# Attention with its probabilities turned by DMA: one transfer per plane for both row tiles, instead of one per plane and tile

## The reference

```python
qkv = mix_precision_matmul(x, weight_qkv)       # x here is layernorm(x)
q, k, v = jnp.split(qkv, 3, axis=-1)
q = q / jnp.sqrt(jnp.asarray(d, dtype=q.dtype))
qk = jnp.einsum('bqd,bkd->bqk', q, k)
s = jax.nn.softmax(qk, axis=-1)
y = jnp.einsum('bqk,bkd->bqd', s, v)
return jnp.matmul(y, out_w.T) + out_b
...
x = x + _layernorm(_L0_attn_ref(_layernorm(x), ...))
x = x + _layernorm(_L0_ffn_ref(_layernorm(x), ...))
```

## Time and profile before

| what | value |
|---|---|
| median of the timed runs | 859.05 us (858.09, 859.05 and one at 1708.93) |
| the profiled execution's own time | 856.61 us |
| its span | 854.8 us |
| granted TensorE clock, mean | 0.976 |
| TensorE, matmuls | 809.6 us busy, 95%, x5870 |
| VectorE | 693.6 us, 81% |
| ScalarE | 503.1 us, 59% |
| GpSimd | 434.0 us, 51% |
| DMA queue of SyncE | 54.8% of 16 engines' span |
| pt_hi<-p_hi, pt_lo<-p_lo | 64 transfers each, 4.5 and 3.7 us from issue to landing (medians) |

### The profile page before, as it was taken

The page is one execution under the profiler, slowest core; times in us unless marked ns, Lnnn a source line. Parts: engine busy times, 40 slices in busy tenths (PEclk is TensorE's granted clock), DMA queues, the critical chain, the costliest instruction groups (busy, mean ns, idle before and its releaser), DMA issues.

```text
span 854.8 us, 16115 instructions
## 1 busy us (share of the span) xinstructions
PE 809.6 (95%) x5870; PEld 614.0 (72%) x5870; DVE 693.6 (81%) x1767; ACT 503.1 (59%) x634; POOL 434.0 (51%) x638
## 2 busy tenths in 40 slices
PE   4779999999999999999999999999999999999963
PEld 3437777777777777777777777777777777778853
DVE  4687798877899888877988888888877777898683
ACT  3275566655566675655676756656766565566532
POOL 1100254655656566556546665564456555645872
PEclk8799999999999999999999999999999999999977
DMA  6568854546656646566455666675435455545301
GB/s 178 112 139 144 177 137 107 125 106 141 148 118 117 142 107 143 117 124 148 106 117 119 142 150 118 124 142 99 106 88 105 113 110 123 125 99 108 79 12 38
DMA packets 336574, 101.58 MB, mean 119 GB/s; under 512 B 310256, under 2 KB 336240, under 8 KB 336496
## 3 DMA queue, kind: packets, MB, share of 16 engines
q1 hardware_dynamic: 336496, 100.56, 54.8%
HBM read 18.75 MB, written 8.39 MB: 32 GB/s over the span
## 4 chain that ended last, share of the span: by engine, by line
PE 88%; DVE 5%; POOL 2%; ACT 1%; issue 1%; DMA 1%; SPq 1%; ACTq 0%; POOLq 0%; DVEq 0%
PE M L885 7%; PE M L886 7%; PE M L887 7%; PE S L917 6%; PE Y L936 6%; PE Y L939 6%; PE Y L937 6%; PE Y L938 6%; PE Y L940 6%; PE S L921 6%; PE S L918 6%; PE S L920 6%; PE S L919 6%; PE M L965 2%; DMA xs<-in_L_attn_x 1%
## 5 line engine op out<-in xcount | busy, mean ns | idle before, releaser
L681 DVE TENSOR_SCALAR_CACHE_REDUCE probs<-S 128x512 f32<-128x512 f32 x256 | 173.0, 679 | 94.9 <-PE S L921 94.4
L514 ACT ACTIVATE probs<-probs,exp_bias,kappa 128x2048 f32<-128x2048 f32 x64 | 134.0, 2094 | 70.7 <-DVE exp_bias L692 70.7
L697 DVE TENSOR_TENSOR p_lo<-probs,p_hi 128x2048 f16<-128x2048 f32 x64 | 166.0, 2594 | 1.9 <-ACT p_hi L475 1.9
L936 PE MATMUL Y<-pt_hi,planes 128*128 128x256 f16 x512 | 139.6, 273 | 0.3 <-issue 0.3
L939 PE MATMUL Y<-pt_lo,planes 128*128 128x256 f16 x512 | 139.6, 273 | 0.0
L937 PE MATMUL Y<-pt_lo,planes 128*128 128x256 f16 x512 | 139.6, 273 | 0.0
L940 PE MATMUL Y<-pt_hi,planes 128*128 128x256 f16 x512 | 139.6, 273 | 0.0
L938 PE MATMUL Y<-pt_hi,planes 128*128 128x256 f16 x512 | 139.6, 273 | 0.0
L475 ACT ACTIVATE p_hi<-probs 128x2048 f16<-128x2048 f32 x64 | 122.0, 1906 | 1.2
L917 PE MATMUL S<-turned,q_hi 128*128 128x512 f16 x256 | 98.8, 386 | 10.3 <-DVE probs L681 7.7
L532 ACT ACTIVATE att<-att,ashift,arstd 128x256 f32<-128x256 f32 x62 | 33.9, 593 | 111.6 <-POOL ashift L387 111.6
(11 more groups left out here) (135 smaller groups left out, 2078.9 us busy)
## 6 DMA issues: line engine op xcount, KB each, us to landing
x_res<-in_L_attn_x SPq DMA_DIRECT2D x32, 256.0 KB, 3.8
out_x<-gate SPq DMA_DIRECT2D x32, 256.0 KB, 3.0
xs<-in_L_attn_x SPq DMA_DIRECT2D x32, 128.0 KB, 3.1
xs<-in_L_attn_x SPq DMA_DIRECT2D x16, 256.0 KB, 4.0
pt_hi<-p_hi SPq DMA_TRANSPOSE x64, 4.5
pt_lo<-p_lo SPq DMA_TRANSPOSE x64, 3.7
pt_hi<-in_L_attn_weight_qkv SPq DMA_DIRECT2D x3, 128.0 KB, 2.8
pt_hi<-in_L_attn_weight_qkv SPq DMA_DIRECT2D x1, 256.0 KB, 3.1
```

What stands on the lines that cost most here:

```text
L681: dve.tensor_scalar(probs[:, t, c * BLK:(c + 1) * BLK], S[k % RING][:, :], 1.0, None, ALU.mult, ALU.max, accum_out=chunk_max[:, t, c:c + 1 ...
L697: dve.tensor_tensor(p_lo[:, t, :], probs[:, t, :], p_hi[:, t, :], ALU.subtract).then_inc(p_lo_made, 1)
L936: pe.matmul(to[:, 0, :], low, p_h, start=first, stop=False, skip_group_check=True)
```

## The change

`turn_probs(h, plane)` turns one plane of both tiles in one transfer of 32 blocks: `p_hi` [128, 2 x 2048] to `pt_hi[:, a]`, and likewise for the low plane. For this the turned planes are laid out tile by tile, [128, 2, 2, 16, 128] with tile before key tile. The high plane's transfer is due in slot 9 and waits for both tiles' p_hi, the low one's in slot 11 as before, waiting for both tiles' p_lo. There is one semaphore per plane. `probs_high` waits for the high plane's transfer of the block before (for either tile), `probs_low` of tile 0 for the low plane's. `attend` waits for both planes, and its moving operand is now two runs of 128 elements, 2048 elements (4 KB) apart.

```diff
-    TURN_P = (7, 11)
+    TURN_P = (9, 11)
...
-        pt_hi = sb("pt_hi", [P, 2, NKT, ROWS], F16)
-        pt_lo = sb("pt_lo", [P, 2, NKT, ROWS], F16)
+        pt_hi = sb("pt_hi", [P, 2, RT, NKT, P], F16)
+        pt_lo = sb("pt_lo", [P, 2, RT, NKT, P], F16)
...
-            def turn_probs(h, t):
-                a, cols = h % 2, slice(t * P, (t + 1) * P)
-                if h == 1 and t == 0:
+            def turn_probs(h, plane):
+
+                a = h % 2
+                if h == 1:
                     sp.wait_ge(w_turned, 7)
-                if h >= 2 and t == 0:
+                if h >= 2:
                     sp.wait_ge(pv_done, h - 1)
-                sp.wait_ge(p_hi_made, h * RT + t + 1)
-                sp.dma_start_transpose(pt_hi[:, a, :, cols], p_hi[:, t, :]).then_inc(pt_in[t], 16)
-                sp.wait_ge(p_lo_made, h * RT + t + 1)
-                sp.dma_start_transpose(pt_lo[:, a, :, cols], p_lo[:, t, :]).then_inc(pt_in[t], 16)
+                if plane == 0:
+                    sp.wait_ge(p_hi_made, (h + 1) * RT)
+                    sp.dma_start_transpose(pt_hi[:, a].rearrange("p t k q -> p (t k) q"),
+                                           p_hi.rearrange("p t n -> p (t n)")).then_inc(pt_hi_in, 16)
+                else:
+                    sp.wait_ge(p_lo_made, (h + 1) * RT)
+                    sp.dma_start_transpose(pt_lo[:, a].rearrange("p t k q -> p (t k) q"),
+                                           p_lo.rearrange("p t n -> p (t n)")).then_inc(pt_lo_in, 16)
...
             def probs_high(h, t):
                 act.wait_ge(exp_made, h * RT + t + 1)
                 if h >= 1:
-                    act.wait_ge(pt_in[t], 32 * h)
+                    act.wait_ge(pt_hi_in, 16 * h)
...
             def probs_low(h, t):
                 dve.wait_ge(p_hi_made, h * RT + t + 1)
+                if h >= 1 and t == 0:
+                    dve.wait_ge(pt_lo_in, 16 * h)
...
-                    for t in range(RT):
-                        pe.wait_ge(pt_in[t], 32 * (h + 1))
+                    pe.wait_ge(pt_hi_in, 16 * (h + 1))
+                    pe.wait_ge(pt_lo_in, 16 * (h + 1))
...
-                p_h, p_l = pt_hi[:, h % 2, kt, :], pt_lo[:, h % 2, kt, :]
+                p_h, p_l = pt_hi[:, h % 2, :, kt, :], pt_lo[:, h % 2, :, kt, :]
```

More of the change, by code:

```diff
@@ L241, in sandwich @@
         exp_made = sem("exp_made"); p_hi_made = sem("p_hi_made"); p_lo_made = sem("p_lo_made")
-        pt_in = [sem(f"pt_in{i}") for i in range(RT)]
+        pt_hi_in = sem("pt_hi_in"); pt_lo_in = sem("pt_lo_in")
         pv_done = sem("pv_done"); y_hi_made = sem("y_hi_made"); y_lo_made = sem("y_lo_made")
@@ L262, in sandwich @@
         waited = sem("waited")
-        stage = f32(pt_hi[:, 1].rearrange("p k q -> p (k q)"))
+        stage = f32(pt_hi[:, 1].rearrange("p t k q -> p (t k q)"))
         stage_qkv = [stage[:, 0:3 * D], stage[:, 3 * D:6 * D]]
-        stage_w = f32(pt_lo[:, 1].rearrange("p k q -> p (k q)")).rearrange("p (w h c) -> p w h c", w=4, h=HALVES)
+        stage_w = f32(pt_lo[:, 1].rearrange("p t k q -> p (t k q)")).rearrange("p (w h c) -> p w h c", w=4, h=HALVES)
         w_half = probs[:, 1, 0:3 * D // 2].bitcast(F16)
```

## The result

The kernel with the merged transfers takes 863.2 us (median of 12 runs, 860.36 to 864.95) where the kernel before takes 857.75 (855.09 to 859.05). The ratio is 1.0067, with a 95% interval of 1.0052 to 1.0083: 4.5 to 7 us slower, which is clear of noise and a third of the 2% that would count. (One run of the kernel before, 1708.93 us, and later one of another kernel, 3536.71, lay far outside and are in no ratio.) The profiled execution took 864.18, with a span of 862.1 against 854.8.

The account below looks back on a forecast made before the run. TensorE, full in the middle, was taken as the bound. 856.6 + 0.5 (first attend) + 1.3 (last attend) = 858.4; as timed runs lie 1.5 to 2.4 above the profiled execution, the forecast was 860.4 us, range 856 to 867.

Parts of the forecast that it names:

- What bounds it: Middle of the run: TensorE is busy 660.00 of 660.00 us, so only longer matmuls or TensorE waits there matter.
- The transfer, 5.5 us: Merged transfer, issue to landing: 1.24 + 2 x 1.81 + 0.64 = 5.5 us, possible from 3.7 to 9.1.
- Full steps, 0: Middle steps: pt_lo lands 1.8 us later, but 5.7 us of slack remain, so no cost.
- Block 2, 0: Short step at the start, h = 2: 7.7 us of room against a 5.5 us landing, no cost; at 9.1, 1.4.
- The first attend, +0.5: Start: the two merged transfers run into each other, pt_lo lands at 61.1, TensorE waits 0.5 us, reaching the end whole.
- The clock, 0, at most 1.5: Last attend's wait: TensorE might then be granted 0.50, costing up to 1.5 us; meant for the range, not the sum.
- The last attend, +1.3: End: the landing comes 1.8 us later, 0.48 is taken in by the wait for GpSimd, 1.3 us reach the end.
- The operand, 0: Matmuls of attend: moving columns in two runs 4 KB apart cost nothing; bounds 2.6 us more or 2.6 less.
- The rate that collapses: Rival: 32-block transfers lose their rate and land late in every step; at 100 GB/s about 969 us; chance 0.04.
- the gap in the operand: Rival: the gap in attend's moving operand costs array time, 6.7 ns on 2560 matmuls, 877 us in all; chance 0.02.
- the undisturbed engines: Rival: fewer, larger transfers disturb the engines less, matmul spacing falls to 0.107, 5 us less, 855; chance 0.02.
- The added waits of ScalarE and VectorE: Each step: p_hi now waits for pt_hi, p_lo for pt_lo of the block before; late only together with TensorE.

Follow-up runs that it names:

- all-apart run: Changed kernel with its new layout, but every block turned tile by tile as before, two transfers of 16 blocks per plane; 858.0 us, ratio 1.0016.
- the kernel before with a filled drain: Kernel before the change, with 28, 22, 26 and 22 unused matmuls before four waits in the drain; 851.66 us, ratio 0.9935.
- only block 31 apart: Changed kernel, but block 31 is turned tile by tile as before the change; 860.54 us, ratio 1.0051 to the kernel before.
- blocks 0 to 2 apart: Changed kernel, but blocks 0, 1 and 2 are turned tile by tile as before the change; 859.46 us, ratio 1.0043 to the kernel before.
- The filled waits: Changed kernel with 18 unused matmuls on TensorE before its waits for the first and last attend; 860.77 us, ratio 1.0039 to the kernel before.
- the second dose: Changed kernel; in blocks 4 to 29, ahead of pt_lo, an extra 32-block transfer, its landing awaited, then a 16-block one; 951.05 us, ratio 1.1104.

## Why the prediction was right, and where its sum was not

The forecast was 860.4 us in a range of 856 to 867 and no change by the 2% bound; 863.2 lies inside. The mechanism held: the middle costs nothing, and what is lost is lost at the two ends. The sum was too small by a factor of about three: I had 1.8 us, the runs show 4.5 to 7. Two things made the number look better than that. The forecast stood on 858.6 for the kernel before, from two timed runs, and the twelve of the comparison give 857.75. And the range had its upper end from landings of 9.1 us, which did not come at the last `attend` (5.6), not from the late arrival and the clock that made the loss. That it held is in part luck, and a bound of 2% is wide for a change of this size.

- *What bounds it.* Right: TensorE, full in the middle in both traces.
- *The transfer, 5.5 us.* Right to a few tenths: 5.5 at the least, medians 5.6 and 5.8. The longest of the new kind was 8.3; my upper end was 9.1. The rate of 288 to 291 GB/s holds through 32 blocks. The Trainium skill (DMA: Bandwidth & Descriptors, "Latency and other measured facts") gives some 350 to 400 GB/s for a DMA transpose in the contiguous case. No run here shows it, if contiguous means the destination: the all-apart run has the old length and no gaps, and its best landing is 3.6 us, as with gaps.
- *Full steps, 0.* Right for the change: the lag stands at 2.75 from block 4 to 30. The slack was overstated. I took 5.7 us, worked out from one step, for all; the quiet steps have it, that very step has 4.70 (its pt_lo took 6.5 us to land), and the tightest middle step has 2.15.
- *Block 2, 0.* Wrong, 0.49 us of wait in the profiled run. I counted the room from the end of p_lo, 7.7 us less the landing. But in the kernel before pt_lo of that block was made at 91.33 and issued only at 92.64, behind x_res, three x loads and pt_hi, and landed 2.45 us before `attend` asked. In the changed kernel it was made at 92.97 and issued at 93.36, right behind the three x loads; its issue took 5.55 us, and it landed 8.2 us after the start of the issue where I had 5.5. The long landing is most of it, SyncE's lateness 0.39 us. I had costed the landing of a transfer that has the list and the DMA engines to itself; what of the 8.2 is the issue and what the loads beside it, no run separates. A transfer of 32 blocks holds SyncE 4.0 us and not twice 1.6, and the loads queue behind it.
- *The first attend, +0.5.* The step that failed most: the start as a whole is worth 0.24 to 0.51%, 2 to 4.4 us. The landing came as computed (9.6 us after pt_hi's issue, 9.2 worked out), but I measured the wait from 60.65, and that arrival of TensorE was itself late: two score tiles at clock 0.50 stood before it. Where the clock was 1.00 there, TensorE arrived at 58.19 (all apart) and 58.22 (the kernel before with a filled drain), and with merged transfers at block 0 it waited 2.26 to 2.36 us in each of four traces. Between the run with only block 31 apart and the all-apart run the first `attend` differs by 1.5 us.
- *The clock, 0, at most 1.5.* The size was right (1.68 at the start), the place and the number were wrong. I meant to count it into the range for the last wait alone (the sum of the upper end, 4.9 + 1.4 + 1, does not even contain it); it follows the first wait in the changed kernel's trace, the last wait in the trace with blocks 0 to 2 apart, and more of the drain runs at 0.50 in the changed kernel's. The filled waits give 0.28% back, 2.4 us, uncertain by about 0.23%. It belonged in the sum, with a probability.
- *The last attend, +1.3.* Right: the start moved by 1.93 (1.8 worked out), and 1.2 of it is left at the next feed (3.95 less 2.75) after the wait on GpSimd has taken its part. The timed runs put the end at 0.16 to 0.43%, 1.4 to 3.7 us, the clock behind it included.
- *The operand, 0.* Right, 0.547 us per key tile in both. What the all-apart run lies over 1.000 (0.0016, its interval beginning at 1.0001) stays open; its trace is longer only in the drain, at the lower clock.
- *Rivals.* The rate that collapses, the gap in the operand and the undisturbed engines are all out. The added waits of ScalarE and VectorE never showed as waits of their own.

## What to carry to other kernels

The longer transfer was hidden in the full middle of this pipeline and bare in its first and last round, so price it there: when was its source made, when is it asked for, and is the asker's arrival in that trace early or late by chance. Read slack in every round and take the smallest, and charge a merged transfer also for the time in which it holds the queue that issues it. Where TensorE waits, add the lower clock that may follow to the price of the wait: with the second dose it followed seven of 26 waits of 1.7 to 5.3 us and cost 1.7 to 2.7 us each time. Unused matmuls in the waits of the drain bought 0.5 to 0.65% here, while no placing of the transfers came out faster than the kernel before. And look at more than one trace of the kernel before: where TensorE arrives at its first `attend` moved by 2.4 us from one to the other.

## What the runs showed of the hardware

- Issuing a DMA transpose of 32 blocks of 128 x 128 held SyncE 4.0 us (3.9 to 5.6), one of 16 blocks 1.3 to 1.6 when the queue was free and up to 4.5 when not: more than twice for twice the size. The data moved at 288 to 291 GB/s for both sizes, with and without gaps in the destination.
- After idle times of 2.0 to 5.3 us TensorE was several times granted its lower level of 1.2 GHz, though not each time: in the run with the second dose behind seven of 26 waits of 1.7 to 5.3 us; behind 2.36 us at the start of the changed kernel and behind 2.28 us at the end of the run with blocks 0 to 2 apart it was, behind 2.29 us at the end of the changed kernel it was not. With unused matmuls in the waits of the drain the mean granted clock rose from 0.978 to 0.996.
